# The last batch of a second top-1 routing, in two groups of two tiles

## What is computed

```
def _top1_router(gate_logits, capacity):
    probs = softmax(gate_logits);  top1 = argmax(gate_logits)
    mask = one_hot(top1, e)
    ranks = cumsum(mask, axis=0) - 1          # over all 4096 tokens, in order
    mask = mask * (ranks < capacity)          # 16 experts, capacity 320
    ...
x = x + 0.5 * ffn(layernorm(x))               # first routing, first experts
x = x + attn(layernorm(x))
x = x + 0.5 * ffn(layernorm(x))               # second routing, second experts
```

## Time and profile before

| | |
|---|---|
| times, three runs | 591.72, 594.5, 596.08 us (median 594.5) |
| the profiled execution | 595.05 us |
| its span, first to last instruction | 593.2 us |
| mean granted TensorE clock | 0.941 |
| TensorE, VectorE, ScalarE, GpSimd busy | 80%, 58%, 53%, 37% |

### The profile page before, as it was taken

The page is one execution under the profiler, slowest core; times in us unless marked ns, Lnnn a source line. Parts: engine busy times, 40 slices in busy tenths (PEclk is TensorE's granted clock), DMA queues, the critical chain, the costliest instruction groups (busy, mean ns, idle before and its releaser), DMA issues.

```text
span 593.2 us, 11158 instructions
## 1 busy us (share of the span) xinstructions
PE 476.7 (80%) x3080; PEld 315.4 (53%) x3083; DVE 346.3 (58%) x1826; ACT 315.2 (53%) x624; POOL 222.0 (37%) x265
## 2 busy tenths in 40 slices
PE   2555389999555789889899999989998954999991
PEld 2444157777323446556565555656565532777770
DVE  2675214343229786878979799788966442234330
ACT  3444134444325467686776867777786530544440
POOL 1577403454734240230605316152122332045555
PEclk9999989999968689999999999999999965999997
DMA  7811434554425100000000000000000012455530
GB/s 240 254 46 48 172 119 145 176 167 145 130 77 194 61 2 2 19 1 2 19 6 23 16 6 28 11 24 11 28 11 28 22 33 61 129 154 173 155 122 34
DMA packets 44841, 45.92 MB, mean 77 GB/s; under 512 B 4936, under 2 KB 34017, under 8 KB 44761
## 3 DMA queue, kind: packets, MB, share of 16 engines
q1 hardware_dynamic: 40184, 37.13, 20.5%
q0 software_dynamic: 4608, 8.22, 4.0%
HBM read 29.61 MB, written 19.17 MB: 82 GB/s over the span
## 4 chain that ended last, share of the span: by engine, by line
PE 46%; DVE 28%; issue 8%; DMA 7%; ACT 5%; POOL 3%; SPq 1%; POOLq 0%; ACTq 0%; DVEq 0%
PE b L612 12%; DVE junk L1192 11%; PE sc L602 11%; PE b L771 3%; PE sc L710 2%; DMA slots<-pay,slot_i 2%; DMA rows<-slots 2%; PE b L682 2%; POOL slots L1341 2%; PE b L591 2%; PE b L626 2%; ACT qT L1007 2%; ACT xn L869 1%; PE b L551 1%; PE b L779 1%
## 5 line engine op out<-in xcount | busy, mean ns | idle before, releaser
L1192 DVE CUSTOM_DVE_ANT_0 junk<-sc,cht 128x256 bf16<-128x256 f32 (+1 forms) x256 | 82.2, 387 | 8.8 <-PE sc L710 7.3
L1341 POOL DMA_INDIRECT slots<-pay,slot_i x64 | 63.8, 996 | 39.1 <-issue 21.1
L913 ACT ACTIVATE hT<-sc 128x320 f32<-128x320 f32 x128 | 56.0, 438 | 39.9 <-PE sc L602 29.1
L612 PE MATMUL b<-hT,w2s 128*128 128x320 f32 x256 | 75.2, 439 | 0.0
L602 PE MATMUL sc<-enT,w1s 128*128 128x320 f32 x256 | 74.4, 435 | 0.5 <-DVE enT L1155 0.4
L1387 POOL COPY vaug<-vall 128x64 f32<-128x64 f32 x32 | 8.4, 266 | 175.7 <-PE b L779 112.2
L771 PE MATMUL b<-probs,vaug 128*32 128x256 f32 x448 | 61.3, 388 | 0.0
L1362 POOL DMA_INDIRECT x<-yrow,ytok x40 | 38.9, 974 | 58.4 <-DVE yrow L1165 48.6
L1147 DVE TENSOR_SCALAR en<-rows 128x128 f32<-128x128 f32 (+1 forms) x80 | 22.5, 367 | 64.4 <-DMA rows<-slots 64.3
L1362 POOL DMA_INDIRECT out<-yrow,ytok x40 | 39.0, 974 | 54.3 <-DVE yrow L1165 44.6
L977 ACT ACTIVATE probs<-sc 128x1024 f32<-128x1024 f32 x48 | 49.1, 1023 | 18.4 <-PE sc L739 18.4
(11 more groups left out here) (142 smaller groups left out, 947.9 us busy)
## 6 DMA issues: line engine op xcount, KB each, us to landing
w1s<-in_L_ffn_w SPq DMA_DIRECT2D x32, 256.0 KB, 3.0
w2s<-in_L_ffn_w SPq DMA_DIRECT2D x32, 256.0 KB, 2.8
slots<-fresh SPq DMA_DIRECT2D x16, 330.0 KB, 4.6
rows<-slots SPq DMA_DIRECT2D x16, 330.0 KB, 3.4
xall<-in_L_attn_x SPq DMA_DIRECT2D x8, 256.0 KB, 4.4
xall<-x SPq DMA_DIRECT2D x8, 256.0 KB, 2.8
out<-xall SPq DMA_DIRECT2D x8, 256.0 KB, 2.3
slots<-pay,slot_i POOLq DMA_INDIRECT x64, 2.3
```

The lines of the kernel that those rows point to most:

```text
L612: last = mm(yps[a], w2s[a][:, f, :], hT[a][:, f, :], start=(f == 0), stop=(f == FC - 1))
L913: nc.scalar.activation(hT[a][:, f, :], hid[f], ACT.Gelu_apprx_tanh).then_inc(e_gelu, 1)
L1192: ins = v.tensor_tensor_reduce(junk[:, H // 2 * h + i, lo:], sc[h][:, i // G, 2 * P * (i % G) + lo:2 * P * (i % G + 1)], tab16["window"][: ...
L1341: gp.indirect_dma_start(out=slots_d[phase], out_offset=bass.IndirectOffsetOnAxis(ap=slot_i[s][:, t:t + 1], axis=0), in_=pay[s][:, t, :], i ...
```

## The change

Steps 8 and 9 are replaced on every engine by a `closing()` with its own order. Batch 7 becomes two groups, LAST = 15 with tiles 28 and 29 and 16 with tiles 30 and 31, each with its own means, root, shift, normalise, transpose, logits, route, ranks, place and scatters, on half-wide slices of the same tiles. The means of the first half come at the end of step 7. Batch 7 uses mv[1] and rstd[1]. Batch 6 has its logits ahead of the sums and values in TensorE's queue, and its ranks between the values of tile 31 and the transpose of tile 30. The new Bank objects put the transposes of batch 7 in sc[1], its logits in sc[0] and the ranks of batch 6 and of both halves in the other bank of sc[0]. Six and two warm-up matmuls into b5 are added. The functions of the routing take a range of tiles `ts`; `sums_copy`, `sinks_copy`, `out_copy` and `r_pay` are the code that stood in ScalarE's step. `last_batch` goes.

More of the change, by code:

```diff
@@ L545, in _, with r_turn @@
             turn(b6[:, 0:E], gw[:, :], ident[0:E, 0:E]).then_inc(gw_turned, 1)
[L547 to L551, removed]
+            def r_turn(g, i, g_of, bank, ps, normed, ts=range(TB)):
+                bank.take(pe, i, r_xnT, lambda i: g_of(i) + 1)
+                for t in ts:
+                    pe.wait_ge(r_xn, normed + (t + 1))
+                    last = turn(ps[:, P * t:P * (t + 1)], xn[:, t, :], ident)
@@ L552, in r_turn, with r_logit @@
                 last.then_inc(r_turned, 1)
-            def r_logit(g, i, g_of, bank, ps):
+            def r_logit(g, i, g_of, bank, ps, ts=range(TB)):
                 pe.wait_ge(r_xnT, g + 1)
                 bank.take(pe, i, r_diff, lambda i: g_of(i) + 1)
-                for t in range(TB):
-                    last = mm(ps[:, E * t:E * (t + 1)], xnT[:, t, :], gwT[:, :], start=(t == 0), stop=(t == TB - 1), skip_group_check=True)
+                for t in ts:
+                    last = mm(ps[:, E * t:E * (t + 1)], xnT[:, t, :], gwT[:, :], start=(t == ts[0]), stop=(t == ts[-1]), skip_group_check=True)
@@ L1023, in step @@
                     if t == 0 and has(b - 2, B):
-                        act.wait_ge(scattered[b % 2], 16 * TB * (4 + (b - 2) // 2))
-                        nc.scalar.copy(pay[b % 2][:, :, 0:D], tiles((b - 2) * TB, TB)).then_inc(r_payx, 1)
+                        r_pay(b - 2)
                         r_exps(b - 2 + B)
-            for b in range(-3, B + 2):
+            def closing():
[17 more added lines that the diff above has]
+                r_pay(B - 1, HALVES[1])
+            for b in range(-3, B):
                 step(b)
+            closing()
             experts(1)
@@ L1065, in means, with shift @@
                 link(ins)
[L1066 to L1072, removed]
+                v.tensor_scalar(ve[:, some], m[:, some, 1], EPS, None, ALU.add).then_inc(done, 1)
+            def shift(m, r, nb, done, ts=range(TB)):
+                some = slice(ts[0], ts[-1] + 1)
+                v.scalar_tensor_tensor(nb[:, some], m[:, some, 0], -1.0, r[:, some], ALU.mult, ALU.mult).then_inc(done, 1)
@@ L1296, in step @@
                     if t == 2:
-                        if has(b - 2, B) and not last_batch(b):
+                        if has(b - 2, B):
                             r_place(b - 2 + B, b % 2)
```

153 lines of the change are left out of this document (88 added, 65 removed).

## The result

The changed kernel takes 590.08 us (median of 15 runs, 585.42 to 592.93), the kernel before 593.81 (15 runs, 591.56 to 596.55). The ratio is 0.9917, with a 95% interval of 0.9895 to 0.9939: faster by 0.8%, or 4.9 us. The forecast was 591.0 in 588.0 to 594.0, "the same" within 1% at 0.84. The sign, the range and the class came out. The gain was forecast at 3.65 us. It is 3.7 between the two medians, 4.9 by the ratio, and 5.6 between the two profiled spans (593.2 and 587.6).

What follows compares the result with a forecast made beforehand. The bound was taken as a serial chain from the last attention tile to the last scatter's landing. The median 594.5 less 3.65 us (2.56 from two scatters, 1.1 from fewer tiles per step) gave 590.9, stated as 591.0, range 588.0 to 594.0.

Steps and rivals of the forecast that it cites:

- Two scatters that no longer stand at the end are 2.56: End of routing: of the 3.65 us gain, 2.56 comes from two scatters no longer standing at the end.
- 95.4: Start of the experts' warm-up to the end of the span: 95.4 us, to stay as long as before within 1 us.
- The late root: GpSimd's reciprocal root for tiles 30 and 31: queued behind three scatters ending at 481.75, it runs 481.9 to 482.95.
- Values 0.99 twice: TensorE, tile 31: the two halves of its values matmuls priced one after the other at 0.99 us each.
- tile 31 is added by 480.3, 0.7 late: Last attention tile's add to x: comes by 480.3, 0.7 us late, from work put in the queues ahead of it.
- rival 1: Clock is full, not half, in the late half (tiles 30, 31): gain 4.45 us, time 590.0; chance 0.2.
- My walk: Each engine's new queue followed from tile 29's add at 471.57, with measured row durations, to the last scatter starting at 491.4.
- The estimate of 33 ns: VectorE routing, late half: 33 ns saved per instruction for 32 fewer elements, 0.3 us in all.
- My own 0.1 in all: VectorE, first maximum to slots, late half: halved width saves 0.1 us in all, taking 3.09 to 3.0.
- Rival 2: Queues eat part of the gain, one late step holding the rest: gain 2.6 or 1.6, 592.0 to 593.0; chance 0.2.
- the lock on shared ports: Within the queue rival: GpSimd scatters each wait for one VectorE instruction; three cost 0.5 to 0.7 us, giving 591.5.
- Rival 3: Experts' start: clock rises only behind the first 16 matmuls, which take 4.55 us longer, giving 595.4; chance 0.05.

Runs made afterwards that it cites:

- the second execution: Changed kernel profiled once more, unaltered, on another chip; last scatter starts 19.99 us after the add of tile 29; that execution took 600.35 us.
- the run with the values apart: Changed kernel with the turn of tile 30's sums moved between the two halves of tile 31's values on TensorE; timed ratio to before 0.9947.
- the two repeated executions: Changed kernel unaltered, profiled again (last scatter 19.99 us after tile 29's add) and timed again (19.18 us, ratio to before 0.9885).
- the whole-batch run: Changed kernel with batch 7 left as one group of four tiles behind the add of tile 31; ratio to before 1.000, median 594.78 us.

## Why the prediction was right, and where its sizes were not

**The mechanism held.** "Two scatters that no longer stand at the end are 2.56": measured 2.55 by stage. Landing and all behind it were as before. The forecast's "95.4" for the stretch from the warm-up to the end was read off a row with only seven of the eight matmuls (497.78); from the first weight load of the warm-up it is 95.8 in both kernels (497.37 and 491.78). The late root stood behind the third scatter of batch 6, as walked, in the first profile. At the half clock the add of tile 31 comes so late that both end together: in the second execution the root starts 0.08 behind the scatter and 1.14 behind the add.

**The values, a term mis-sized.** "Values 0.99 twice" was a sum where the two halves run at once: 1.02 together. That let the slots of batch 6 come at 4.73 where I had 5.8, the third scatter and with it the root 1.06 earlier, and it turned "tile 31 is added by 480.3, 0.7 late" into 0.6 early against the anchor (7.49, before 8.05). By the run with the values apart, it is 1.1 us of the end result at the full clock.

**The clock, a step too narrow.** I priced the clock for the late half alone (0.8 us, rival 1) and took it as full up to 478 in any execution. It is a property of the execution over the whole closing part: 17.7, 19.2 and 20.0 us for one kernel. My walk, full up to 7 and half from there, gave 19.83. It came near the executions at the half clock (19.99), because 16 values matmuls take 1.88 there where I had summed 1.98 at the full clock: two errors that cancel. So that the median's gain (3.7) is so near the forecast one (3.65) is in part luck; by stage single executions differ by 2.3 us.

**Small sizes.** The root of two columns takes 0.72 to 0.76, not the 1.05 of four which I kept (1.05): 0.3. From the first maximum to the slots it is 2.69 (484.71 to 487.40), not 3.0: a 128x32 instruction takes 0.19 where the 128x64 one took 0.22, so nine save 0.3. The estimate of 33 ns for each, worked out from the cost per element in the Trainium skill, "VectorE: DVE Perf Modes", section "The TRN2 errata — SBUF-src ops pay a fixed extra latency per instruction", agrees with the trace (0.03). My own 0.1 in all was the worse number.

**Rival 2**, queues that eat part of it, did not come at the full clock: no step was later than walked. But the margin that it names, VectorE's shift behind the early half's placing, was used up at the half clock: the shift starts 0.31 and 0.32 behind the root's end in the two repeated executions, and 0.03 in the first profile. A scatter beside a busy VectorE took 0.97 (478.61 and 479.89). The 1.03 to 1.04 that the prediction also put there stands at the first scatter behind a root, with VectorE busy (477.27) or idle (481.81). So the lock on shared ports that the Trainium skill names ("SBUF — State Buffer", section "SBUF: two separate sides") shows no price in this kernel; by that page only VectorE instructions in a two-port mode or with two SBUF inputs take it. **Rival 3** did not come: the first 16 matmuls took 4.50.

**The class.** A gain of 3.65 would have been 0.6%; the 0.8% measured stayed inside 1%.

## What to carry to other kernels

When a serial end (here routing plus an indirect scatter for each tile) waits for the last tile of a group, cut the group and not the chain: two groups of two took 5.2 us off between executions whose clock fell at the same places, of which 2.55 are two scatters that now run beside the routing of the last two tiles. Price matmuls with narrow stationary operands by their neighbours and not alone, since two groups on different output rows ran in the time of one; but do not move them together where the second one covers a hand-over, for that made the kernel 2% slower than before the change and took the whole gain with it. Before you move one step off an engine's queue, look for what stands next: the root ahead of the third scatter gained 0.54 us and lost half of it behind VectorE's placing. And when a stretch has TensorE at the edge of a change of clock, take more than one profile of each kernel before you put a microsecond down to a step.

## What was not expected of the hardware

- Matmuls with a 128*32 operand, 8 in 0.99 us; 16, of two halves on different rows of the bank, in 1.02 us at 2.4 GHz and 1.88 at 1.2 GHz (from their start to the sink values). Apart they take 0.99 each at 2.4 GHz.
- The place where the granted clock falls varied by 11 us over three executions of the same program (1.0, 1.2 and 11.9 us behind the add of tile 29). In the whole-batch run it fell inside 475 to 476, after PE had been busy for all of 469 to 473, 0.70 of 473 and 0.93 of 474:

```profile
472.00:473.00 1.00, 1.00 (x9) 0.83 (x7) 0.00 (x0) 0.98 (x4) 0.70 (x2) 1.00 0.04 15
473.00:474.00 1.00, 0.70 (x6) 0.39 (x4) 0.29 (x1) 0.60 (x2) 0.68 (x1) 1.00 0.14 46
474.00:475.00 1.00, 0.93 (x9) 0.96 (x10) 0.00 (x0) 0.40 (x2) 0.00 (x0) 1.00 0.15 53
475.00:476.00 1.00, 1.00 (x11) 0.55 (x15) 0.76 (x4) 0.34 (x2) 0.00 (x0) 0.66 0.06 16
```

  So the clock fell here with PE recorded as busy. What keeps it up is left open.
- GpSimd's power of a 128x2 tile takes 0.72 to 0.76 us and of a 128x4 one 1.05: by an estimate from these two, about 0.15 us for each column, over a fixed 0.4. The first scatter behind such a root takes 1.03 to 1.04 us, the next ones 0.97 to 0.98.
